# Attention row maxima taken over two PSUM banks at a time, score blocks computed in pairs

## The reference, cut to what matters

```python
c6 = silu(c) @ Wc + bc                       # six modulation rows per sequence
sh_msa, sc_msa, g_msa, sh_mlp, sc_mlp, g_mlp = split(c6, 6)
xm = ln(x) * (1 + sc_msa) + sh_msa
q, k, v = xm @ Wq + bq, xm @ Wk + bk, xm @ Wv + bv       # 16 heads of 16
w = softmax((q / 16) @ k.T)                  # 512 x 512 for each head
x = x + g_msa * ((w @ v) @ Wo + bo)
xm2 = ln(x) * (1 + sc_mlp) + sh_mlp
x = x + g_mlp * (gelu(xm2 @ W1 + b1) @ W2 + b2)
```

## Time and profile before

| | |
|---|---|
| median of 3 runs | 859.71 us (859.09, 863.22, 859.71) |
| span of the profiled execution, first to last instruction | 857.3 us (its own time is not recorded apart; the median run is 2.4 us above the span) |
| PE matmuls | 725.0 us busy, 85% |
| DVE | 582.5 us busy, 68%; 335.9 us of it the 512 row maxima |
| ACT | 384.3 us busy, 45% |
| mean granted TensorE clock | 0.906 of 2.4 GHz |

### The profile page before, as it was taken

One profiled execution on the slowest core, in us unless ns is written; L12 is line 12 of the kernel. 1 busy time (PEld: TensorE's weight loads), 2 busy tenths in 40 slices (PEclk: granted clock), 3 DMA queues, 4 the chain that ended last, 5 costly groups with the idle time before them and its releaser, 6 DMA issues.

```text
span 857.3 us, 11761 instructions
## 1 busy us (share of the span) xinstructions
PE 725.0 (85%) x3967; PEld 390.6 (46%) x3967; DVE 582.5 (68%) x1015; ACT 384.3 (45%) x462; POOL 222.2 (26%) x163
## 2 busy tenths in 40 slices
PE   4648589865999599995999599997999798999987
PEld 1531122422247432682257522682258422851776
DVE  5728588863987488874987388875987587560373
ACT  0410156303763177423763167424762376269321
POOL 4262001200316103430315103430325030331244
PEclk9775599956999899997999799998999899899998
DMA  7499700295018910395028910393028611111210
GB/s 262 121 122 161 117 14 26 95 160 94 25 52 152 143 53 25 125 136 113 26 70 143 138 52 25 129 145 100 26 88 148 107 45 36 43 63 37 65 31 24
DMA packets 68774, 75.87 MB, mean 88 GB/s; under 512 B 6214, under 2 KB 59996, under 8 KB 68716
## 3 DMA queue, kind: packets, MB, share of 16 engines
q1 hardware_dynamic: 68716, 75.10, 43.5%
HBM read 49.35 MB, written 25.48 MB: 87 GB/s over the span
## 4 chain that ended last, share of the span: by engine, by line
issue 36%; PE 30%; DVE 11%; POOL 10%; DMA 7%; SPq 3%; ACT 2%; POOLq 0%; DVEq 0%; ACTq 0%
PE ps L616 6%; PE ps L594 6%; PE ps L624 5%; DVE mx L895 5%; PE ps L549 4%; POOL hl L442 4%; PE ps L755 3%; DMA qst<-mrow 3%; SPq L322 3%; DMA kst<-parts_scratch 2%; POOL prob L435 2%; PE ps L759 2%; ACT prob L497 1%; POOL x L415 1%; POOL xd L428 1%
## 5 line engine op out<-in xcount | busy, mean ns | idle before, releaser
L895 DVE TENSOR_REDUCE mx<-ps 128x1 f32<-128x512 f32 x512 | 335.9, 686 | 83.8 <-PE ps L594 80.0
L497 ACT ACTIVATE prob<-ps 128x1024 f32<-128x1024 f32 x256 | 247.9, 1022 | 237.4 <-PE ps L624 237.0
L594 PE MATMUL ps<-kst,qst 96*128 96x512 bf16 x512 | 201.5, 417 | 33.9 <-DVE mx L895 17.5
L624 PE MATMUL ps<-qst,kst 98*128 98x512 bf16 x512 | 156.9, 402 | 60.6 <-DMA qst<-mrow 52.9
L594 PEld LDWEIGHTS ps<-kst,qst 96*128 96x128 bf16 x512 | 46.1, 99 | 204.0 <-DVE mx L895 166.7
L616 PE MATMUL ps<-prob,vaug 128*32 128x512 f32 x1024 | 137.3, 608 | 0.4 <-ACT prob L497 0.3
L442 POOL TENSOR_TENSOR hl<-z,hh 128x512 fp32r<-128x512 f32 x64 | 82.3, 1286 | 138.6 <-DVE hh L1024 138.6
L624 PEld LDWEIGHTS ps<-qst,kst 98*128 98x128 bf16 x512 | 48.8, 102 | 130.1 <-DMA qst<-mrow 54.2
L536 ACT ACTIVATE z<-ps,bias_t 128x512 f32<-128x512 f32 x64 | 44.0, 688 | 135.7 <-PE ps L759 130.1
L390 POOL TENSOR_TENSOR rstd<-vare,mhalf 128x4 f32<-128x4 f32 x16 | 16.3, 1021 | 330.4 <-DVE vare L835 330.4
L549 PE MATMUL ps<-w_hi,hh 128*128 128x256 f32 x256 | 73.6, 287 | 0.3 <-POOL hl L442 0.3
(11 more groups left out here) (106 smaller groups left out, 858.6 us busy)
## 6 DMA issues: line engine op xcount, KB each, us to landing
parts_scratch<-prob SPq DMA_DIRECT2D x32, 384.0 KB, 2.6
qst<-parts_scratch SPq DMA_DIRECT2D x48, 256.0 KB, 11.2
kst<-parts_scratch SPq DMA_DIRECT2D x48, 256.0 KB, 17.6
y_scratch<-rb SPq DMA_DIRECT2D x32, 256.0 KB, 2.0
xa<-in_x_dram SPq DMA_DIRECT2D x8, 512.0 KB, 9.4
xd<-in_x_dram SPq DMA_DIRECT2D x8, 512.0 KB, 3.5
yc<-y_scratch SPq DMA_DIRECT2D x16, 256.0 KB
rb<-r_scratch SPq DMA_DIRECT2D x16, 256.0 KB
```

Source lines behind the costliest of these rows:

```text
L497: act.activation(prob[:, s % 2, 2 * p:2 * p + 2, :], ps[:, 2 * p:2 * p + 2, :], ACT.Exp, scale=1.0 / DH).then_inc(exp_done, 1)
L594: pe.matmul(ps[:, banks[n % len(banks)], :], qst[1 - par][0:MROW, h, t * P:(t + 1) * P], kst[1 - par][0:MROW, h, :], start=True, stop=True ...
L624: m = pe.matmul(ps[:, q, :], kst[par][0:KROWS, G * g + q, kt * P:(kt + 1) * P], qst[par][0:KROWS, G * g + q, :], start=True, stop=True)
L895: dve.tensor_reduce(mx[:, t, h:h + 1], ps[:, banks[n % len(banks)], :], AXX, ALU.max).then_inc(max_done, 1)
```

## The change

A score block becomes a pair: two matmuls write banks 6 and 7, and one `tensor_reduce` over 128 x 2 x 512 writes two columns of maxima. With banks 6 and 7 both in one pair, `banks` is `(6,)`, and pair n waits for the maximum of pair n-1. The counts of blocks become counts of pairs (32 for a sequence) and are redistributed: `C_BLOCKS` alternates one and two. At i = -1 the pairs alternate between banks 6, 7 and 0, 1. At i = 0 every C step has two pairs, both behind `pv`.

```diff
-C_BLOCKS = (1, 0) + (3,) * (STEPS - 4) + (4, 4)
-TURN_BLOCKS, QK_BLOCKS, V_BLOCKS = (1, 1), (0, 1, 0, 1), (0, 1, 0, 1)
-UP_BLOCKS, DOWN_BLOCKS = (1, 1, 1), (2, 2, 2, 2, 2, 0, 0, 0)
-HALF, EXTRA = NH * TT // 2, 8
-OLD_BLOCKS = (4,) * 6 + (0,) * (STEPS - 6)
-NEW_BLOCKS = (0,) * 6 + (4,) * (STEPS - 6)
+NBLOCK = NH * TT // 2
+C_BLOCKS = (1, 0) + (1, 2) * ((STEPS - 4) // 2) + (2, 2)
+TURN_BLOCKS, QK_BLOCKS, V_BLOCKS = (1, 0), (0, 1, 0, 0), (0, 1, 0, 0)
+UP_BLOCKS, DOWN_BLOCKS = (1, 1, 0), (1, 1, 1, 1, 0, 0, 0, 0)
+HALF, EXTRA = NBLOCK // 2, 4
+OLD_BLOCKS = (2,) * 6 + (0,) * (STEPS - 6)
+NEW_BLOCKS = (0,) * 6 + (2,) * (STEPS - 6)
...
-            def scores(i, par, blocks, banks=(6, 7)):
+            def scores(i, par, blocks, banks=(6,)):
...
-                    h, t = n // TT, n % TT
+                    h, first = n // 2, n % 2 * 2
                     if n >= len(banks):
-                        pe.wait_ge(max_done, 64 * (i + 1) + n - len(banks) + 1)
+                        pe.wait_ge(max_done, NBLOCK * (i + 1) + n - len(banks) + 1)
...
-                    pe.matmul(ps[:, banks[n % len(banks)], :], qst[1 - par][0:MROW, h, t * P:(t + 1) * P], kst[1 - par][0:MROW, h, :],
-                              start=True, stop=True).then_inc(s_done, 1)
+                    for t in (first, first + 1):
+                        m = pe.matmul(ps[:, banks[n % len(banks)] + t - first, :], qst[1 - par][0:MROW, h, t * P:(t + 1) * P],
+                                      kst[1 - par][0:MROW, h, :], start=True, stop=True)
+                    m.then_inc(s_done, 1)
...
-                            if later(i, 0, 1):
-                                between(p, p + 1)
-                            elif p == 1:
-                                between(0, 2)
+                            if later(i, 0, 1) and p == 0:
+                                between(0, 1)
                         if s:
                             pv(i, par, s - 1)
-                        between(2, old + new)
+                        between(1 if later(i, 0, 1) else 0, old + new)
...
-                    scores(i, par, HALF + 2, (6, 7, 0, 1))
+                    scores(i, par, HALF + 1, (6, 0))
                     turn_maxima(i, 0, NH // 2, half_turned, 4)
-                    scores(i, par, EXTRA - 2)
+                    scores(i, par, EXTRA - 1)
...
-                    dve.tensor_reduce(mx[:, t, h:h + 1], ps[:, banks[n % len(banks)], :], AXX, ALU.max).then_inc(max_done, 1)
+                    h, first, bank = n // 2, n % 2 * 2, banks[n % len(banks)]
+                    dve.tensor_reduce(mx[:, first:first + 2, h], ps[:, bank:bank + 2, :], AXX, ALU.max).then_inc(max_done, 1)
```

More of the change, by code:

```diff
@@ L46 @@
 QK_BANKS = (4, 5, 2, 3)
-C_BLOCKS = (1, 0) + (3,) * (STEPS - 4) + (4, 4)
-TURN_BLOCKS, QK_BLOCKS, V_BLOCKS = (1, 1), (0, 1, 0, 1), (0, 1, 0, 1)
-UP_BLOCKS, DOWN_BLOCKS = (1, 1, 1), (2, 2, 2, 2, 2, 0, 0, 0)
-assert sum(map(sum, (C_BLOCKS, TURN_BLOCKS, QK_BLOCKS, V_BLOCKS, UP_BLOCKS, DOWN_BLOCKS))) == NH * TT
-HALF, EXTRA = NH * TT // 2, 8
-OLD_BLOCKS = (4,) * 6 + (0,) * (STEPS - 6)
-NEW_BLOCKS = (0,) * 6 + (4,) * (STEPS - 6)
+NBLOCK = NH * TT // 2
+C_BLOCKS = (1, 0) + (1, 2) * ((STEPS - 4) // 2) + (2, 2)
+TURN_BLOCKS, QK_BLOCKS, V_BLOCKS = (1, 0), (0, 1, 0, 0), (0, 1, 0, 0)
+UP_BLOCKS, DOWN_BLOCKS = (1, 1, 0), (1, 1, 1, 1, 0, 0, 0, 0)
+assert sum(map(sum, (C_BLOCKS, TURN_BLOCKS, QK_BLOCKS, V_BLOCKS, UP_BLOCKS, DOWN_BLOCKS))) == NBLOCK
+HALF, EXTRA = NBLOCK // 2, 4
+OLD_BLOCKS = (2,) * 6 + (0,) * (STEPS - 6)
+NEW_BLOCKS = (0,) * 6 + (2,) * (STEPS - 6)
 OLD_TURN = 5
-assert HALF + EXTRA + sum(OLD_BLOCKS) == NH * TT and OLD_TURN < STEPS // 2
+assert HALF + EXTRA + sum(OLD_BLOCKS) == NBLOCK and OLD_TURN < STEPS // 2
 WO_AT, LN2_AT, TURN_AT = 2, 5, 5
@@ L239, in tail_blocks @@
             new = NEW_BLOCKS if isinstance(i, int) and i == 0 else C_BLOCKS
-            return NH * TT - sum(map(sum, (new, TURN_BLOCKS, QK_BLOCKS, V_BLOCKS)))
+            return NBLOCK - sum(map(sum, (new, TURN_BLOCKS, QK_BLOCKS, V_BLOCKS)))
         def early(i):
@@ L580, in _ @@
             block_at = [0]
-            def scores(i, par, blocks, banks=(6, 7)):
+            def scores(i, par, blocks, banks=(6,)):
                 for _ in range(blocks if runs(i, 1) else 0):
                     n = block_at[0]
-                    block_at[0] = (n + 1) % (NH * TT)
-                    h, t = n // TT, n % TT
+                    block_at[0] = (n + 1) % NBLOCK
+                    h, first = n // 2, n % 2 * 2
                     if n >= len(banks):
-                        pe.wait_ge(max_done, 64 * (i + 1) + n - len(banks) + 1)
+                        pe.wait_ge(max_done, NBLOCK * (i + 1) + n - len(banks) + 1)
                     elif n == 0:
@@ L593, in scores @@
                             pe.wait_ge(mrow_done, 2 * (i + 1))
-                    pe.matmul(ps[:, banks[n % len(banks)], :], qst[1 - par][0:MROW, h, t * P:(t + 1) * P], kst[1 - par][0:MROW, h, :],
-                              start=True, stop=True).then_inc(s_done, 1)
+                    for t in (first, first + 1):
+                        m = pe.matmul(ps[:, banks[n % len(banks)] + t - first, :], qst[1 - par][0:MROW, h, t * P:(t + 1) * P],
+                                      kst[1 - par][0:MROW, h, :], start=True, stop=True)
+                    m.then_inc(s_done, 1)
             def turn_maxima(i, first=0, last=NH, turned=mt_done, bank=6):
                 if runs(i, 1):
-                    pe.wait_ge(max_done, 64 * (i + 1) + TT * last)
+                    pe.wait_ge(max_done, NBLOCK * (i + 1) + 2 * last)
                     if bank == 4:
@@ L882, in _, with row_max @@
             block_at = [0]
-            def row_max(i, blocks, banks=(6, 7)):
+            def row_max(i, blocks, banks=(6,)):
                 if not runs(i, 1):
@@ L889, in row_max @@
                     n = block_at[0]
-                    block_at[0] = (n + 1) % (NH * TT)
+                    block_at[0] = (n + 1) % NBLOCK
                     if n == 0 and later(i, 1, 1):
                         dve.wait_ge(mt_done, i + 1)
-                    dve.wait_ge(s_done, 64 * (i + 1) + n + 1)
-                    h, t = n // TT, n % TT
-                    dve.tensor_reduce(mx[:, t, h:h + 1], ps[:, banks[n % len(banks)], :], AXX, ALU.max).then_inc(max_done, 1)
+                    dve.wait_ge(s_done, NBLOCK * (i + 1) + n + 1)
+                    h, first, bank = n // 2, n % 2 * 2, banks[n % len(banks)]
+                    dve.tensor_reduce(mx[:, first:first + 2, h], ps[:, bank:bank + 2, :], AXX, ALU.max).then_inc(max_done, 1)
             def z_hi(n, b):
@@ L1053, in step @@
                     if early(i):
-                        row_max(i, HALF + 2, (6, 7, 0, 1))
+                        row_max(i, HALF + 1, (6, 0))
                         maxima_rows(i, NH // 2, half_turned, half_rows, 4)
-                        row_max(i, EXTRA - 2)
+                        row_max(i, EXTRA - 1)
                     else:
```

## The result

The changed kernel takes **945.67 us** (median of 4 runs, 937.87 to 951.18); the kernel before, run again beside it, 861.47. The ratio is **1.094**, 95% interval 1.089 to 1.100: 84 us slower. Forecast were 931 us, 71 us slower, range 905 to 968.

The account below looks back on a forecast made before the run. PE, without slack in the C stages, was taken to bound the kernel. Terms of 47.4 + 19.8 + 2 + 1 + 0.5 + 0.3 = 71 us on 859.7 gave 931 us, range 905 to 968 (forecast mechanism's own range 915 to 950).

Parts of the forecast that it names:

- PE bounds the C stage: C stages before the change: PE busy 4.00 of 4.00 us without slack; DVE returns each bank before PE needs it.
- A pair comes back after 1.93 us: Start of one pair to earliest start of the next: 0.22 + 0.43 + 1.22 + 0.06 = 1.93 us.
- Seven waits of 1.06 in each later C stage: C stages of i = 1 to 6: PE waits 1.06 us seven times, 7.4 us a stage; 47.4 us in six with start effects.
- Steps of 4.33 at i = 0: C stage of i = 0: both pairs behind `pv`, steps 4.33 instead of 3.09 us; 1.24 more, 16 times, 19.8 us.
- 2 us for the clock: C stage of i = 0: PE's clock rises from 0.50 one step later, costing 2 us (0 to 5).
- the first rival: C stage of i = 0: clock stays at 0.50, steps of 6.9 us, 36 us more, total 967; chance 0.08.
- my argument against the rival: Against a clock staying low at i = 0: PE works 5.4 us without a gap in each such step.
- Q/K stage, nothing: Q/K stage: DVE's 0.54 us delay is covered by a held cast; 0, bounds -0.6 and +0.6 for each of five.
- Tail of i = 0, 1.5 us: From the C stage of i = 0 to the next: 1 us for the tail (0 to 5), 0.5 for Q/K.
- Loads: First load to next C stage, i = 1 to 5: MLP delays vanish in the wait of about 9 us; difference 0.
- The later clock rival: Later C stages: clock falls, half of each stage's time low, 14 us more six times, total 1015; chance 0.05.
- The six parts: Forecast differences by stretch of the timeline: +47.4, +21.8, +1.5, 0, 0 and +0.3 us.

Follow-up runs that it names:

- run 2: Kernel before, each reduction reading only 64 of the 512 columns of its bank: 827.2 us.
- Run 1: Changed kernel, each reduction reading only 64 of the 512 columns of either bank: 836.3 us, ratio 0.965 to the kernel before.
- run 6: Changed kernel, from i = 1 on mostly one pair in a C step, the pairs taken out moved into the MLP: 875.1 us, ratio 1.014.
- Run 3: Changed kernel's pair places, but each matmul and each reduction over 512 has its own count and waits only for its own bank: 913.8 us, ratio 1.057.
- run 5: Changed kernel plus 12 matmuls with overwritten results in PE's idle time before the C stage of i = 0: 935.1 us, ratio 1.084.
- run 4: Changed kernel, at i = 0 one pair between the halves of the transposed scores and one behind `pv`: 931.1 us, ratio 1.076.

## Why the prediction came out right, point by point

- **PE bounds the C stage.** Right: with short reductions the stage did not get shorter (run 2).
- **A pair comes back after 1.93 us.** Right to the hundredth (458.44 to 460.37), and nearly so the reduction, 1.223 against 1.225. Run 1 removes the length and with it the loss. PE's idle time in front of pairs is 87.5 us, where about 65 were named as a sign; 17.5 of it was there before.
- **Seven waits of 1.06 in each later C stage, 47.4 us in six.** Right: 48.9. The stages differ: 7.4 to 8.2 us more at i = 1, 2, 3, 5 and 6, but 9.7 at i = 4. At the stage's start I had 0.78 for the second pair. In the stage of 446.77 the transposed scores in front of it begin at 452.77, so PE could have issued it at 453.20; it starts at 454.08, 0.88 late.
- **Steps of 4.33 at i = 0, and 2 us for the clock.** The step is right, the clock is the term that was mis-sized: 30.5 us for the stage against 21.8 in the profiled execution. I took one more slow step. This execution had six from 98.86 to 140.53: a first one of 4.87, which has no `pv`, and five of 6.89, which is the price that the first rival gave (6.9). So that rival happened in part. In each of the five PE worked 5.57 us without a gap (6.89 less 1.32), so my argument against the rival did not hold here. Nor is the late rise a fixed price of the change: run 6, with the same code at i = 0, was at 1.00 from about 107 and had 73.0 us, 17.2 more than before and less than the 21.8 forecast. What decides between an early and a late rise stays open. The four runs of the changed kernel spread over 13 us, as much as the two stages differ; that the clock at i = 0 makes this spread is likely but not shown, since one of them was profiled.
- **Q/K stage, nothing.** Wrong by 0.7 us a stage, 3.5 in five, just past the bound of 0.6. The cast of the earlier trace rows doesn't cover it all. Run 3 has the same 0.6 more with single reductions, so most of it comes from where the blocks now stand and not from the longer reduction.
- **Tail of i = 0, 1.5 us.** 4.4, within the bounds given (0 to 5 for the tail, and 0.5 for the Q/K stage). 3.2 of it lie between the first load and the next stage, where executions scatter: run 5 had 3.0 more there than the kernel before, runs 4 and 6 had 0.2 more and 0.2 less.
- **Loads.** I had them at no difference; in the profiled execution they took 6.4 us longer in five stages. From the first load to the next stage it is 29.2 to 33.4 us in the kernel before alone, and 27.4 to 34.5 in the single and pair kernels with full reductions that wait for them, so this is no effect of the change that can be told from noise.
- **The later clock rival.** It did not come as priced, with the clock low for half of each stage. In the C stages of i = 1 to 6 the clock is at 0.50 in the first 3 to 6 us, as before the change (4 to 6), then at 1.00 with PE at 3.48 of 4.00, with one exception: at i = 4 the second pair waited 2.37 us (to 558.69), its reduction having started late, and the clock was at 0.50 from about 559.6 to 563.0 (0.57 in the stretch from 559 to 563). The late pair and the slow stretch are why that stage lost 9.7 us and the others 7.4 to 8.2. The Trainium skill's rule on micro-idle PE under cycling PSUM banks ("TensorE: Matmul & The Clock Gate", "A second HAM failure mode: psum-queue depth-cycling") is not borne out by the regular waits of about 1 us, of which there are seven in each of these stages; the one fall followed a longer one. What i = 0 shows is a clock that was low already and rose late.
- **Was the total luck?** Little of it. The six parts are off by +1.5, +8.7, +2.9, +3.5, +6.4 and -1.9 us, so hardly anything cancels; they add up to the 21 us by which the profiled execution is above the forecast of 71. The median is 14.7 above the 931 forecast, inside the own range of 915 to 950.

## What to carry to other kernels

Before two small reductions are joined, compare two lengths: the time from writing a buffer to having it back, and the other work that the writing engine has between two writes. Joining used up both PSUM banks, and the return went from 1.18 to 1.93 us against 0.87 us of work: 0.15 us saved at an engine off the path cost 1.06 on it, seven times a stage. If work must wait for a DMA anyway, move movable work there: 14 blocks taken out of each full stage gave 1.4%, and with three more out of the way to the loads it was 5%, with the blocks as they were; more than half of the second step is not explained. And where a phase's time depends on when the clock rises, profile more than one execution before a difference there is put down to the code.

## What the runs showed of the hardware that I had not expected

One `tensor_reduce` over two banks of PSUM costs 1.223 us, over one 0.686, over 2 x 64 columns 0.293, so its length goes by elements with some 0.15 us fixed. The clock of TensorE stayed at half for 44 us of work (98.9 to about 143) while PE worked in stretches of 5.6 us with holes of 1.3 us between; in run 6 the same instructions in the same stage had it rise at about 107, in run 4 with the holes elsewhere at about 110. What makes the difference stays open; the runs of run 5 spread over 28 us. A single wait of 2.4 us in a stage at full clock was followed by 3.4 us at half (at i = 4), the regular ones of about 1 us in the stages of i = 1 to 6 were not. Runs 3 and 5 have one such fall of 3.4 us each in the stage of i = 0 (from 126.5 and from 125.2).
